# Second attention of a two-layer transformer kernel: softmax row sums taken beside the exponentials, 16 reciprocals a row, and two steps of VectorE's order moved

## The chip, the cores and the metric

One Trainium2 chip, one of its cores. The metric is the device time of one execution in microseconds (us); smaller is better. The kernel before was timed three times: 2356.11 us in the median, 2355.34 the lowest and 2362.7 the highest.

## The reference

Two layers work on 2048 tokens of 512 channels, each layer an attention and a feed-forward, each with a layer norm modulated by a conditioning vector. The first feed-forward is a mixture of 64 experts, 8 of them per token. The change is in the attention of the second layer:

```python
# q: 16 heads of 32; k, v: 4 heads of 32, each shared by 4 query heads; q and k get a rotary embedding
for qs in range(0, S, WINDOW):            # WINDOW = 128 queries
    # keys: 16 meta tokens, and the window of 128 positions up to the query
    scores = einsum('bhqd,bhkd->bhqk', q_c, k_c) * scale
    scores = where(allowed, scores, -inf)
    attn = softmax(scores, axis=-1)
    chunks.append(einsum('bhqk,bhkd->bhqd', attn, v_c))
...
return y @ Wo + bo
```

The softmax is computed as exp(s - max) and divided by its sum over the keys. All is float32.

## The kernel before, in words

The kernel is one program of several stages; the second attention is a block of its own between two barriers. It works on 16 tiles ("rows") of 128 tokens. Each engine has a hand-written program with one function `turn` that `schedule(turn)` (L1369) calls 22 times, once per m from -4 to 17. In turn m seven different rows are in work at once: `g=m+4` gathers the expert outputs from memory, `y=m+3` adds them to the residual `x_res` and takes the statistics of the layer norm, `p=m+2` is normalised and projected, `f=m+1` has its queries and keys transposed, `s=m` gets scores, masks, minima and exponentials, `a=m-1` has its probabilities transposed and multiplied with the values, `w=m-2` is normalised by the row sums, projected by Wo and added to the residual. A row index outside 0 to 15 is None and its part is left out. There is no planner: within a turn each engine runs its list in the order written, and semaphores tie the engines together.

VectorE (L1714), per turn: `xhat` (L1720, needs GpSimd's 1/sqrt of the variance, L1457); the normalisation of row w (L1725 a RECIPROCAL of the 128x512 sums from PSUM, L1727 the product with the output, which gives `o_out`); quarter 0 of the minima of row s (`maxima(s,0)`, four L1690 and one L1694, which writes the differences for the meta keys); the keys' copy (L1737); three experts added (L1701); the query bias (L1746, waits for the projection, gives `q_rows`); quarter 1; two experts; the bias of keys and values (L1756, L1758); quarter 2; three experts; the residual sum of row w (L1767, `x_out`); quarter 3; the statistics of row y (L1703: L1708, L1710, L1712, each behind a small memset, L1656).

GpSimd (L1454), per turn: L1457; the modulation of h (L1417 and L1461, gives `h_done`); L1465 (`x_res` plus bias); gathers of three experts of row g (each L1445, an indirect DMA that GpSimd issues, behind one small L1422); the rotary embedding of the queries (L1417, L1437; waits for `q_rows`); two gathers; the rotary embedding of the keys; three gathers. Before each group of gathers it waits for `y_sum`, that is until VectorE has added the same experts of the row before (L1442), because they are read from the same buffer.

TensorE (L1559), per turn: scores of quarter 0 (L1546); the transposes of h (L1569, wait for `h_done`) and of the queries (L1576); the transposes of the probabilities of quarter 0 of row a (L1556, wait for `o_out`, since they use the banks that held the output and the sums); the query projection (L1590, its end starts L1746); scores 1, transposes 1, key and value projection (L1599), scores 2, transposes 2, the Wo projection (L1610), transposes 3, scores 3, the transposes of the meta probabilities (L1622), the transposes of the keys (L1630, wait for `x_out`), and last the two products of row a: values times probabilities into bank `b_o`, ones times probabilities (the row sums, spread over 32 partitions per head) into bank `b_sum`. Each product is 8 matmuls of 512 columns (L1639) and 16 of 128 columns (L1643); the second set has the same shapes and another left operand.

ScalarE (L1501) copies PSUM to SBUF (hT L1506, qT L1511, the transposed probabilities L1499, the meta ones L1518, kT L1528) and takes the exponentials, 16 per row of 256 columns (L1492), after each quarter of the minima, and one for the meta keys (L1534). SyncE loads the tables of the rotary embedding (L1409) two rows ahead.

Of the kernel before, what the change touches and what calls it, by code (L numbers as in the profile page):

```python
# [5 lines left out]
ALU = mybir.AluOpType  # L6
# [103 lines left out]
def adaln_two_layers(nc, a, out):  # L110
    ctx = ExitStack()
    with ctx:
# [1207 lines left out]
        with ExitStack() as ph, nc.Block() as block:  # L1320
# [17 lines left out]
            meta_sum = cv(HP, 2, HD)  # L1338
            ones_f = cv(HD)
# [6 lines left out]
            nmx = cv(2, NHEAD)  # L1346
            spare = cv(2)
            free = mod[:, 0].rearrange("p j c -> p (j c)")
            oT, osum = free[:, 0:C].rearrange("p (r n) -> p r n", r=HP), free[:, C:2 * C]
# [8 lines left out]
                     "exp_done", "meta_exp", "pT_mm", "pT_out", "pM_mm", "pM_out", "o_mm", "o_out", "wo_mm", "x_pre", "x_out",  # L1358
# [3 lines left out]
             exp_done, meta_exp, pT_mm, pT_out, pM_mm, pM_out, o_mm, o_out, wo_mm, x_pre, x_out,  # L1362
# [3 lines left out]
            ba, bb, b_o, b_sum = psum[6], psum[7], psum[4], psum[5]  # L1366
# [48 lines left out]
            def _(pool):  # L1415
# [34 lines left out]
                st.did(nc.gpsimd.memset(ones_f, 1.0))  # L1450
# [33 lines left out]
            def _(act):  # L1484
                copy = nc.scalar.copy

                def exps(t, c):
                    for r in range(HP):
                        n = HP * c + r
                        act.wait_ge(mx_done, NHEAD * t + n + 1)  # L1490
                        some = slot(t, c)[:, r, META:KEYS1]
                        nc.scalar.activation(some, some, ACT.Exp, bias=nmx[:, t % 2, n:n + 1], scale=-1.0).then_inc(exp_done, 1)  # L1492
# [8 lines left out]
                def turn(g, y, p, f, s, a, w):  # L1501
                    if p is not None:
# [35 lines left out]
            def _(pe):  # L1538
# [20 lines left out]
                def turn(g, y, p, f, s, a, w):  # L1559
                    if s is not None:  # L1560
                        scores(s, 0)
                    if p is not None:
# [3 lines left out]
                        if a:  # L1566
                            pe.wait_ge(pM_out, a)
# [10 lines left out]
                    if f == 0:  # L1578
                        pe.wait_ge(spread_done, 1)
                        pe.wait_ge(kv_rows, 1)  # L1580
                        nc.tensor.matmul(b_sum[:, 0:NKV1 * HD], spread, v[0:META, 0].rearrange("p h d -> p (h d)"), start=True, stop=True).then_inc(meta_mm, 1)
# [34 lines left out]
                    if a is not None:  # L1616
                        pe.wait_ge(meta_exp, a + 1)
                        pe.wait_ge(kv_rows, p + 1 if p is not None else NT)
                        if a:
                            pe.wait_ge(pM_out, a)  # L1620
                        for n in range(2):
                            mm = nc.tensor.transpose(bb[:, n * P:(n + 1) * P], prob_meta[:, a % 2, HM * n:HM * n + HM].rearrange("p h k -> p (h k)"), ident[:])  # L1622
                        mm.then_inc(pM_mm, 1)
# [8 lines left out]
                    if a is not None:  # L1632
                        pe.wait_ge(pT_out, copies_before(a + 1, 0))
                        pe.wait_ge(pM_out, a + 1)
                        for bank, local, meta in ((b_o, lambda k, c: v[:, keys_of(a, k) % VRING, c], lambda r, c: v_meta[:, c // 2, r, c % 2]),
                                                  (b_sum, lambda k, c: ones_f, lambda r, c: meta_sum[:, r, c % 2])):
                            for k in chunks(a):
                                for c in range(NKV1):
                                    nc.tensor.matmul(bank[HD * c:HD * c + HD], local(k, c), probT[:, k, c].rearrange("p r n -> p (r n)"),  # L1639
                                                     start=(k == 0), stop=False)  # L1640
                            for r in range(HP):
                                for c in range(NKV1):
                                    mm = nc.tensor.matmul(bank[HD * c:HD * c + HD, r * P:(r + 1) * P], meta(r, c), metaT[:, c // 2],  # L1643
                                                          start=False, stop=(r == HP - 1))
                                    if r == HP - 1:
# [539 lines left out]
```

## Time and profile before

| | us |
|---|---|
| median of 3 runs (lowest, highest) | 2356.11 (2355.34, 2362.7) |
| the profiled execution, its own time | 2370.22 |
| its span in the profile | 2366.9 |
| second attention, from its first xhat to its last residual sum | 1241 to 1775 |
| TensorE busy over the span | 2059.5 (87%) |
| VectorE, GpSimd, ScalarE busy over the span | 1122.9, 726.6, 708.0 |
| mean granted TensorE clock, share of 2.4 GHz | 0.935 |

The table is read from the page of the profile (its first part has the busy times) and from the timelines of the block. A busy share averages over stages with different limits, so this case is read row by row inside the one stage: which wait ends last in a row, and what the engine that ended it had been doing. "Idle before <- X" in a line names the instruction whose end released the wait. A wait marked "issue" ended with nothing that the profile can name; where a semaphore had several sources it can still be one of them, and the ends of the other engines' instructions show which. Granted clock 1.00 is 2.4 GHz, 0.50 is 1.2 GHz.

### The profile page before, as it was taken

The page shows a single profiled execution, that of the slowest core. Times are in us where ns is not written, and L with a number is a line of the kernel's source. Part 1 is how long each engine was busy: PE and PEld are TensorE (multiplying, and loading weights), DVE is VectorE, ACT ScalarE, POOL GpSimd, SP SyncE. Part 2 cuts the span into 40 slices and gives each one's busy share as a digit, 9 for nine tenths or more (in the row PEclk, how much of TensorE's full clock was granted, in tenths as well). Part 3 has the DMA queues.
Part 4 walks back from the last instruction along what each step waited for, and adds up shares of the span by engine and source line. Part 5 has one row for each costly group of instructions (what it writes and reads, how often), then busy time and mean ns, then how long its engine had stood idle before and what let it go on. Part 6 is the DMA issues. An engine that isn't in the chain of part 4 may idle for free. (4 is left out here: it accounts for less than half of the span.)

```text
span 2366.9 us, 39347 instructions
## 1 busy us (share of the span) xinstructions
PE 2059.5 (87%) x11764; PEld 1340.5 (57%) x11766; DVE 1122.9 (47%) x2920; ACT 708.0 (30%) x1455; POOL 726.6 (31%) x1164
## 2 busy tenths in 40 slices
PE   4799877999999999999933788888875999999998
PEld 2677544555555555555511445545543878878787
DVE  2466666555553222222225677777534444443432
ACT  0233235222222222222200444444522332232221
POOL 0243302223333333233337666666302101101000
PEclk7799889999999999999966799999987999999999
DMA  7565632566555566656552222222002112121210
GB/s 249 178 212 202 218 115 81 190 197 196 181 192 189 181 220 201 212 183 220 166 164 74 74 74 74 79 73 71 1 1 72 63 62 72 63 80 62 80 63 27
DMA packets 122555, 302.36 MB, mean 128 GB/s; under 512 B 24912, under 2 KB 28624, under 8 KB 122320
## 3 DMA queue, kind: packets, MB, share of 16 engines
q1 hardware_dynamic: 73424, 179.04, 22.4%
q0 software_dynamic: 23040, 75.52, 11.4%
q10 hardware_dynamic: 25984, 46.38, 5.3%
q8 instruction: 67, 1.10, 0.2%
q14 instruction: 40, 0.33, 0.0%
HBM read 216.47 MB, written 83.36 MB: 127 GB/s over the span
## 5 line engine op out<-in xcount | busy, mean ns | idle before, releaser
L1166 PE MATMUL bank<-arena 128*128 x1272 | 445.6, 494 | 9.9 <-issue 8.8
L1166 PEld LDWEIGHTS bank<-arena 128*128 128x128 f32 x1272 | 229.6, 190 | 147.6 <-issue 16.9
L1183 PE MATMUL bank<-arena 96*128 x632 | 297.5, 593 | 0.2 <-issue 0.2
L1287 DVE TENSOR_TENSOR arena<-bank,mod 128x512 f32<-128x512 f32 x158 | 109.2, 691 | 215.4 <-PE bank L1183 176.7
L1881 PE MATMUL bank<-x_hi,w_hi 128*128 128x512 f32 x512 | 200.9, 392 | 6.0 <-DVE x_lo L2014 6.0
L1881 PE MATMUL bank<-x_hi,w_lo 128*128 128x512 f32 x512 | 199.4, 389 | 0.0
L1881 PE MATMUL bank<-x_lo,w_hi 128*128 128x512 f32 x512 | 199.2, 389 | 0.0
L1282 DVE TENSOR_TENSOR arena<-arena,bank 128x192 f32<-128x192 f32 x159 | 56.3, 354 | 300.9 <-ACT arena L1204 300.4
L1199 ACT COPY arena<-bank 96x256 f32<-96x256 f32 x158 | 58.1, 368 | 424.0 <-issue 221.9
L1145 POOL DMA_INDIRECT arena<-h_moe,arena x160 | 158.2, 989 | 75.3 <-issue 74.0
L1144 POOL TENSOR_TENSOR arena<-neg_half 128x1 f32<-128x1 f32 x160 | 31.4, 196 | 462.8 <-PE bank L1175 462.6
L2094 DVE SCALAR_TENSOR_TENSOR ffn_arena<-bank,ffn_arena,mod 128x512 f32<-128x512 f32 x64 | 48.0, 751 | 221.3 <-PE bank L1881 174.3
L1183 PEld LDWEIGHTS bank<-arena 96*128 96x128 f32 x632 | 107.3, 190 | 76.4 <-issue 76.4
L1445 POOL DMA_INDIRECT route_hot<-y_moe,pos_u x128 | 125.5, 981 | 32.1 <-issue 27.9
L1701 DVE SCALAR_TENSOR_TENSOR x_res<-route_hot,route_w,x_res 128x512 f32<-128x512 f32 x128 | 115.4, 902 | 25.5 <-DMA route_hot<-y_moe,pos_u 17.7
L1862 POOL TENSOR_TENSOR ffn_arena<-ffn_arena,neg_half 128x1 f32<-128x1 f32 x16 | 8.8, 548 | 386.3 <-DVE ffn_arena L2028 386.3
L1492 ACT ACTIVATE arena<-arena 128x256 f32<-128x256 f32 x256 | 109.2, 502 | 18.7 <-DVE arena L1690 18.6
L1175 PEld LDWEIGHTS bank<-ident,arena 128*128 128x128 f32 x640 | 80.2, 141 | 58.9 <-issue 28.7
L1881 PEld LDWEIGHTS bank<-x_hi,w_hi 128*128 128x128 f32 x512 | 96.1, 188 | 29.0 <-issue 4.8
L1556 PE MATMUL bank<-ident,arena 128*128 128x128 f32 x496 | 78.4, 309 | 34.3 <-issue 31.9
L1881 PEld LDWEIGHTS bank<-x_hi,w_lo 128*128 128x128 f32 x512 | 96.1, 188 | 20.2
L1881 PEld LDWEIGHTS bank<-x_lo,w_hi 128*128 128x128 f32 x512 | 96.2, 188 | 19.4
(318 smaller groups left out, 3679.4 us busy)
## 6 DMA issues: line engine op xcount, KB each, us to landing
arena<-in_moe_up SPq DMA_DIRECT2D x64, 768.0 KB, 7.9
y_moe<-arena ACTq DMA_DIRECT2D x158, 256.0 KB, 2.9
y_moe<-mod SPq DMA_DIRECT2D x32, 1024.0 KB
ffn_arena<-in_ffn_up SPq DMA_DIRECT2D x64, 512.0 KB, 3.3
arena<-in_moe_down SPq DMA_DIRECT2D x64, 384.0 KB, 9.9
arena<-in_L_wmod SPq DMA_DIRECT2D x12, 1024.0 KB, 6.5
x_res<-in_L_attn_x SPq DMA_DIRECT2D x1, 4096.0 KB
h_moe<-arena SPq DMA_DIRECT2D x16, 256.0 KB, 7.3
```

The costliest lines, as they stand in the source:

```text
L1145: nc.gpsimd.indirect_dma_start(out=xg[:, b], out_offset=None, in_=h_moe, in_offset=bass.IndirectOffsetOnAxis(ap=st_tok[:, b], axis=0)).the ...
L1166: mm = nc.tensor.matmul(psum[2 + b][:, 0:2 * FI], xgT[:, b, k], up_ring[:, bass.ds((e % RING) * UPW + k * 2 * FI, 2 * FI)], start=(k == 0) ...
L1175: mm = nc.tensor.transpose(psum[b][:, k * P:(k + 1) * P], xg[:, b, k * P:(k + 1) * P], ident[:])
L1183: mm = nc.tensor.matmul(psum[6 + b][:], hiddenT[:, b, n], down_ring[:, bass.ds((e % RING) * DOWNW + n * C, C)], start=(n == 0), stop=(n == 1))
L1199: nc.scalar.copy(hiddenT[:, b], psum[4 + b][0:FH, 0:2 * P].rearrange("p (n q) -> p n q", n=2)).then_inc(hT_out, 1)
L1282: nc.vector.tensor_tensor(hidden[:, b], gate_act[:, b], psum[2 + b][:, FI:2 * FI], ALU.mult).then_inc(hidden_done, 1)
L1287: nc.vector.tensor_tensor(y[:, b], psum[6 + b][:], mod[:, 0, 5], ALU.mult).then_inc(y_out, 1)
L1445: nc.gpsimd.indirect_dma_start(out=yg[:, j], out_offset=None, in_=y_moe, in_offset=bass.IndirectOffsetOnAxis(ap=pos_u[:, t, j:j + 1], axis ...
L1492: nc.scalar.activation(some, some, ACT.Exp, bias=nmx[:, t % 2, n:n + 1], scale=-1.0).then_inc(exp_done, 1)
L1556: mm = nc.tensor.transpose(psum[4 + k][:, r * P:(r + 1) * P], slot(t, c)[:, r, at:at + P], ident[:])
L1701: nc.vector.scalar_tensor_tensor(x_res[:, t], yg[:, j], route_w[:, t, j:j + 1], x_res[:, t], ALU.mult, ALU.add).then_inc(y_sum, 1)
L1881: mm = nc.tensor.matmul(bank, x, y, start=(n == 0), stop=(n == len(passes) - 1))
```

## The change

Six edits, all in the block of the second attention:

1. TensorE no longer computes the row sums: the second product (8 L1639 and 16 L1643 a row) is gone, with the tiles `ones_f` and `meta_sum`.
2. ScalarE's exponentials give their sum along the keys through `accum_out` into `esum`, 16 a row.
3. VectorE has a new step `sums(a)` between the query bias and quarter 1: a reduce of the meta probabilities (128x256 to 128x16), an add of 128x16 and a reciprocal of 128x16, which gives `r_done`. Row w loses its 128x512 reciprocal.
4. The 16 reciprocals a token are turned by one more TensorE transpose (into the bank of the meta transposes), copied by ScalarE (`rT`), spread by four TensorE matmuls with a selection matrix `sel` (16 partitions, 128 columns each) into bank `b_r` ahead of the product with the values, and copied by ScalarE into `rb` at the start of the next turn. L1727 then multiplies the output with `rb`.
5. VectorE's residual sum of row w (L1767) stands before the last three experts and no longer behind them.
6. The statistics of row y stand before quarter 3 of the minima and no longer behind it.

Cut to its core:

```diff
@@ ScalarE
                 def exps(t, c):
+                    if t >= 2 and c == 0:
+                        act.wait_ge(r_done, t - 1)
...
-                        nc.scalar.activation(some, some, ACT.Exp, bias=nmx[:, t % 2, n:n + 1], scale=-1.0).then_inc(exp_done, 1)
+                        nc.scalar.activation(some, some, ACT.Exp, bias=nmx[:, t % 2, n:n + 1], scale=-1.0,
+                                             accum_out=esum[:, t % 2, n:n + 1]).then_inc(exp_done, 1)
...
                 def turn(g, y, p, f, s, a, w):
+                    if w is not None:
+                        act.wait_ge(o_mm, 2 * NKV1 * w + HP)
+                        if w:
+                            act.wait_ge(o_out, w)
+                        copy(rb, b_r[:]).then_inc(rb_out, 1)
...
                                 act.wait_ge(pM_mm, a + 1)
+                                copy(rT, bb[0:NHEAD, 2 * P:3 * P]).then_inc(pM_out, 1)
@@ TensorE
+                        pe.wait_ge(r_done, a + 1)
+                        nc.tensor.transpose(bb[0:NHEAD, 2 * P:3 * P], rinv, ident[:]).then_inc(pM_mm, 1)
...
-                        for bank, local, meta in ((b_o, lambda k, c: v[:, keys_of(a, k) % VRING, c], lambda r, c: v_meta[:, c // 2, r, c % 2]),
-                                                  (b_sum, lambda k, c: ones_f, lambda r, c: meta_sum[:, r, c % 2])):
+                        for r in range(HP):
+                            nc.tensor.matmul(b_r[:, r * P:(r + 1) * P], sel[:, r], rT, start=True, stop=True).then_inc(o_mm, 1)
...
@@ VectorE
+                def sums(t):
+                    dve.wait_ge(meta_exp, t + 1)
+                    dve.wait_ge(exp_done, NHEAD * t + NHEAD)
+                    if t:
+                        dve.wait_ge(pM_mm, t)
+                    st.did(nc.vector.tensor_reduce(msum, prob_meta[:, t % 2], AX.X, ALU.add))
+                    st.settle()
+                    st.did(nc.vector.tensor_tensor(msum, msum, esum[:, t % 2], ALU.add))
+                    st.settle()
+                    nc.vector.reciprocal(rinv, msum).then_inc(r_done, 1)
...
-                        st.did(nc.vector.reciprocal(osum, b_sum[:]))
-                        st.settle()
-                        nc.vector.tensor_tensor(oT.rearrange("p r n -> p (r n)"), b_o[:], osum, ALU.mult).then_inc(o_out, 1)
+                        dve.wait_ge(rb_out, w + 1)
+                        nc.vector.tensor_tensor(oT.rearrange("p r n -> p (r n)"), b_o[:], rb, ALU.mult).then_inc(o_out, 1)
...
+                    if a is not None:
+                        sums(a)
                     if s is not None:
                         maxima(s, 1)
...
                     if s is not None:
                         maxima(s, 2)
-                    if y is not None:
-                        for j in range(5, TOPK):
-                            add_expert(y, j)
                     if w is not None:
                         dve.wait_ge(wo_mm, w + 1)
                         dve.wait_ge(x_pre, w + 1)
                         nc.vector.tensor_tensor(x_res[:, w], ba[:], x_res[:, w], ALU.add).then_inc(x_out, 1)
+                    if y is not None:
+                        for j in range(5, TOPK):
+                            add_expert(y, j)
+                    if y is not None:
+                        statistics(y)
                     if s is not None:
                         maxima(s, 3)
-                    if y is not None:
-                        statistics(y)
```

Once per execution, `sel` is filled by a VectorE copy of 512 columns, and the copy of as many columns that filled `meta_sum` is gone.

## Rows read from the trace of the kernel before

**Rows 1.** Windows, one for each row between two L1746; engine busy (instructions), clock, DMA share, GB/s.

```profile
1361.94:1391.56 29.62, 24.85 (x202) 14.29 (x203) 22.34 (x58) 13.15 (x29) 19.41 (x24) 0.94 0.27 74
...
1624.79:1653.26 28.47, 25.02 (x202) 14.83 (x203) 21.91 (x58) 13.21 (x29) 19.49 (x23) 0.94 0.28 77
```

**Rows 2.** VectorE timeline, one row: start, us, instruction, [idle before <- what released it].

```profile
1506.22 0.69 DVE L1746 TENSOR_TENSOR arena<-bank,arena 128x512 f32<-128x512 f32 x1 [1.23 <-PE bank L1590]
...
1508.55 2.17 DVE L1694 TENSOR_TENSOR mod<-arena 128x64 f32<-128x64 f32 x1
...
1517.92 0.68 DVE L1767 TENSOR_TENSOR x_res<-bank,x_res 128x512 f32<-128x512 f32 x1
...
1526.53 3.36 DVE L1725 RECIPROCAL mod<-bank 128x512 f32<-128x512 f32 x1 [2.72 <-PE bank L1643]
```

**Rows 3.** TensorE timeline of the same row.

```profile
1518.75 0.63 PE L1630 MATMUL bank<-ident,arena 128*128 128x128 f32 x4 [2.10 <-DVE x_res L1767]
...
1530.71 1.94 PE L1556 MATMUL bank<-ident,arena 128*128 128x128 f32 x8 [2.64 <-issue]
```

**Rows 4.** GpSimd timeline of the same row.

```profile
1518.80 0.19 POOL L1422 TENSOR_TENSOR arena<-neg_half 128x1 f32<-128x1 f32 x1
...
1525.25 1.27 POOL L1461 TENSOR_TENSOR down_scale<-down_scale,mod 128x512 f32<-128x512 f32 x1
```

**Rows 5.** Timeline, VectorE, GpSimd and TensorE, an early row without residual sum.

```profile
1328.13 1.12 PE L1569 MATMUL bank<-ident,down_scale 128*128 128x128 f32 x4 [5.67 <-POOL down_scale L1461]
...
1335.05 0.69 DVE L1746 TENSOR_TENSOR arena<-bank,arena 128x512 f32<-128x512 f32 x1 [4.18 <-PE bank L1590]
...
1344.83 0.43 DVE L1690 CUSTOM_DVE_ANT_0 arena<-bank,mask 128x272 f32<-128x272 f32 x1
...
1345.30 0.46 POOL L1437 TENSOR_TENSOR arena<-arena,mod 128x128 f32<-128x128 f32 x1
...
1353.46 1.11 PE L1569 MATMUL bank<-ident,down_scale 128*128 128x128 f32 x4 [1.57 <-POOL down_scale L1461]
```

**Rows 6.** Timeline, the next row: VectorE's L1694 beside GpSimd's pair of L1417.

```profile
1363.77 1.65 POOL L1417 TENSOR_TENSOR mod<-arena 128x256 f32<-128x256 f32 x2
...
1364.26 1.25 DVE L1694 TENSOR_TENSOR mod<-arena 128x64 f32<-128x64 f32 x1
```

**Rows 7.** Timeline, late rows, without gathers: TensorE, VectorE, GpSimd.

```profile
1668.90 1.27 POOL L1461 TENSOR_TENSOR down_scale<-down_scale,mod 128x512 f32<-128x512 f32 x1
...
1673.94 1.94 PE L1556 MATMUL bank<-ident,arena 128*128 128x128 f32 x8 [2.62 <-issue]
...
1690.87 1.92 PE L1639 MATMUL bank<-arena 128*32 128x512 f32 x16
...
1695.17 1.08 PE L1643 MATMUL bank<-arena 128*32 128x128 f32 x32
...
1696.37 3.36 DVE L1725 RECIPROCAL mod<-bank 128x512 f32<-128x512 f32 x1 [4.51 <-PE bank L1643]
...
1764.89 3.36 DVE L1725 RECIPROCAL mod<-bank 128x512 f32<-128x512 f32 x1 [6.75 <-PE bank L1643]
```

**Rows 8.** Groups of instructions that come nearest to the added ones.

```profile
L1233 DVE TENSOR_REDUCE arena<-arena 128x4 f32<-128x256 f32 x16 | 6.7, 421 | 0.5
...
L700 DVE RECIPROCAL arena<-bank 128x8 f32<-128x8 f32 x32 | 4.4, 179 | 2.1 <-PE bank L595 2.1
...
L691 DVE TENSOR_TENSOR route_w<-arena 128x16 f32<-128x16 f32 x8 | 1.3, 167 | 0.0
...
L1492 ACT ACTIVATE arena<-arena 128x256 f32<-128x256 f32 x256 | 109.2, 502 | 18.7 <-DVE arena L1690 18.6
...
L1518 ACT COPY arena<-bank 128x256 f32<-128x256 f32 x16 | 6.0, 373 | 5.5 <-PE bank L1622 5.0 <-issue 0.4
```

**Rows 9.** Timeline, TensorE: matmuls from 16 partitions, and of 256 columns.

```profile
1275.83 0.79 PE L1581 MATMUL bank<-arena 16*128 16x128 f32 x2
...
1507.72 1.89 PE L1599 MATMUL bank<-arena,mod 128*128 128x256 f32 x8
```

More of the change, by code:

```diff
@@ L1345, in adaln_two_layers @@
             st1, r1 = cv(8), cv(2)
-            nmx = cv(2, NHEAD)
+            nmx, esum = cv(2, NHEAD), cv(2, NHEAD)
+            msum, rinv = cv(NHEAD), cv(NHEAD)
+            rT, sel = cv(P)[0:NHEAD], cv(HP, P)[0:NHEAD]
             spare = cv(2)
             free = mod[:, 0].rearrange("p j c -> p (j c)")
-            oT, osum = free[:, 0:C].rearrange("p (r n) -> p r n", r=HP), free[:, C:2 * C]
+            oT = free[:, 0:C].rearrange("p (r n) -> p r n", r=HP)
+            rb = free[:, C:2 * C]
             hT = free[:, 2 * C:3 * C].rearrange("p (k n) -> p k n", k=KC)
@@ L1580, in turn @@
                         pe.wait_ge(kv_rows, 1)
-                        nc.tensor.matmul(b_sum[:, 0:NKV1 * HD], spread, v[0:META, 0].rearrange("p h d -> p (h d)"), start=True, stop=True).then_inc(meta_mm, 1)
+                        nc.tensor.matmul(b_r[:, 0:NKV1 * HD], spread, v[0:META, 0].rearrange("p h d -> p (h d)"), start=True, stop=True).then_inc(meta_mm, 1)
                     if a is not None:
@@ L1633, in turn @@
                         pe.wait_ge(pT_out, copies_before(a + 1, 0))
-                        pe.wait_ge(pM_out, a + 1)
-                        for bank, local, meta in ((b_o, lambda k, c: v[:, keys_of(a, k) % VRING, c], lambda r, c: v_meta[:, c // 2, r, c % 2]),
-                                                  (b_sum, lambda k, c: ones_f, lambda r, c: meta_sum[:, r, c % 2])):
[L1637 to L1645, printed above, removed]
-                                        mm.then_inc(o_mm, 1)
+                        pe.wait_ge(pM_out, 2 * a + 2)
+                        for r in range(HP):
+                            nc.tensor.matmul(b_r[:, r * P:(r + 1) * P], sel[:, r], rT, start=True, stop=True).then_inc(o_mm, 1)
+                        for k in chunks(a):
+                            for c in range(NKV1):
+                                nc.tensor.matmul(b_o[HD * c:HD * c + HD], v[:, keys_of(a, k) % VRING, c], probT[:, k, c].rearrange("p r n -> p (r n)"),
+                                                 start=(k == 0), stop=False)
+                        for r in range(HP):
+                            for c in range(NKV1):
+                                mm = nc.tensor.matmul(b_o[HD * c:HD * c + HD, r * P:(r + 1) * P], v_meta[:, c // 2, r, c % 2], metaT[:, c // 2],
+                                                      start=False, stop=(r == HP - 1))
+                                if r == HP - 1:
+                                    mm.then_inc(o_mm, 1)
                 schedule(turn)
@@ L1661, in weights_ready @@
                     st.did(nc.vector.tensor_tensor(bo, bo, mod[:, 1, 2], ALU.mult))
+                    st.did(nc.vector.tensor_copy(sel.rearrange("n r (c d) -> n r c d", c=NKV1),
+                                                 ident[0:NHEAD, 0:NHEAD].rearrange("n (c r) -> n r c", r=HP).unsqueeze(3).to_broadcast([NHEAD, HP, NKV1, HD])))
                     nc.vector.tensor_copy(spread.rearrange("p (h k) -> p h k", h=HM),
@@ L1670, in meta_values @@
                     head = meta_head.rearrange("p (c r) -> p r c", c=2).unsqueeze(3).to_broadcast([P, HP, 2, HD])
-                    st.did(nc.vector.tensor_copy(meta_sum[:], head))
                     dve.wait_ge(meta_mm, 1)
                     for n in range(2):
-                        rows = b_sum[:, n * 2 * HD:(n + 1) * 2 * HD].rearrange("p (c d) -> p c d", c=2)
+                        rows = b_r[:, n * 2 * HD:(n + 1) * 2 * HD].rearrange("p (c d) -> p c d", c=2)
                         st.did(nc.vector.tensor_tensor(v_meta[:, n], rows.unsqueeze(1).to_broadcast([P, HP, 2, HD]), head, ALU.mult))
```

16 lines of the change are left out of this document (6 added, 10 removed).

## The prediction, made before the result was known

> **What bounds the kernel now.** I first cut the block into rows of work, from one start of the query bias L1746 to the next, and asked for busy times [rows 1]. The 10 rows from 1361.94 to 1653.26 take 291.3 us, 29.13 each. No engine is busy all the time: TensorE some 25 us, VectorE 22, GpSimd 19, ScalarE 13. So a row is bound by a chain that hops between engines, and a removed instruction is worth what it had on that chain. The clock column is 0.94 to 1.00.
>
> The timelines of one row show the chain [rows 2 to 4]. VectorE reaches L1767 at 1517.92, behind three experts; TensorE had waited 2.10 us for it before the keys' transposes at 1518.75; both products follow; at 1526.53 VectorE starts the 3.36 us reciprocal, after 2.72 us of waiting for the products. TensorE's next transposes start at 1530.71 after 2.64 us of idle that the view calls "issue"; the end of L1727 (right behind the reciprocal, 0.7 us) is what they waited for. Then come the query projection and the next L1746. Beside it runs a second chain: GpSimd issues three gathers from 1518.80 and finishes the modulated h at 1525.25 + 1.27 = 1526.52 [rows 4]. That is just when the products end. That is the point of this case: who comes second decides what the removal is worth.
>
> The early rows, before any output exists, show the second chain alone [rows 5]. From h at 1328.13 TensorE needs 6.92 us to the query bias at 1335.05; VectorE has added its last expert at 1344.83; GpSimd ends the keys' rotation at 1345.76, gathers, and h of the next row is there at 1353.46. That is 25.3 us with no reciprocal in it, with half the transposes of a full row.
>
> After 1653 there are no gathers, and the rows are bound by TensorE and the reciprocal [rows 7].
>
> **Part by part.** All sums are against the profiled execution, 2370.22 us (span 2366.9). It is 14.1 above the median of 2356.11; I take the differences over unchanged.
>
> Removed: the reciprocal, 3.36 plus some 0.04 of settling, 3.4 a row on VectorE. The second product: both take 1695.17 + 1.08 - 1690.87 = 5.4 us undisturbed [rows 7], half of it, 2.6 to 2.7, goes; in rows with gathers the same stretch lasts from 1519.3 to 1526.5, 7.2 [rows 2, 3], so up to 1 us more may go there.
>
> Added on TensorE: one transpose and four matmuls from 16 partitions. L1581 is that kind: 2 instructions of 128 columns in 0.79 at the 1.2 GHz level [rows 9]. L1599, at 2.4 GHz, has 8 of 256 columns in 1.89, so 8 of 128 take 0.9. Bounds 0.9 and 1.6; I take 0.9, as the stretch runs mostly at 2.4 GHz. The products become 0.9 + 2.6 = 3.5 instead of 5.4.
>
> Added on ScalarE: a copy of 128 columns ahead of the meta one. L1518, twice as wide, takes 0.37 [rows 8], so 0.25; it lies on the path to the products, which hence gain 1.9 - 0.3 = 1.6, I take 1.5. A copy of 512 columns at the turn's start, 0.6, is hidden in the 28 us row with 13 busy. The sums of the 16 exponentials: the trace has no activation with an accumulator. VectorE's own read of one costs 0.08; the exponential takes 0.50. Bounds 0 and 0.4 each; I take 0.15, 2.4 us a row, nearest VectorE's read. That is hidden with gathers; in the late rows it makes the exponentials catch up with the transposes' copies, some 0.6 in two rows.
>
> Added on VectorE: sums(a), 0.42 + 0.17 + 0.18 [rows 8] and settling, 0.9. It has a second price. It starts right after L1746, when GpSimd begins its pair of L1417, and its add reads two SBUF operands like L1694. L1694, alone some 0.2 as L691, took 1.25 there and ended with the pair at 1365.5 [rows 6], 2.17 in another row [rows 2]. So I let the add wait until the pair ends: 1.8 for sums(a), bounds 0.9 and 2.8. The Trainium skill, in SBUF (State Buffer), section "Who interferes with whom", says that a VectorE instruction with two SBUF inputs blocks on a GpSimd one that reads SBUF, that the holder keeps the port for one whole instruction, and that a reduce never contends. The trace agrees on who contends, but L1694 was held over two instructions, not one; by the rule sums(a) would cost 1.1 and the total would be some 7 us lower. The measurement decides.
>
> Moved: L1767 before the last three experts. It would be ready earlier by three experts, but TensorE's other work (scores 3, meta transposes) ends 2.10 before it gets L1767's result [rows 3], so 2.1 at most is gained on that chain. And the last three experts, with them GpSimd's last three gathers, come later by L1767's 0.7. The statistics before quarter 3 gain nothing with gathers, as L1457 stands behind the gathers in GpSimd's queue. Behind sums(a) in VectorE's queue stand quarter 1, 5 experts and L1767, so the gathers are late by 1.8 more. SyncE's queue isn't touched; the sel copy replaces the meta_sum copy, 0.
>
> **The sum, rows with gathers.** First chain: L1746 to the end of the products was 1526.5 - 1506.2 = 20.3; now 20.3 - 2.0 - 1.5 = 16.8, then L1727 0.7, transposes 1.9 and projection 3.8, twice L1599 [rows 3, 9]: 23.2. Second chain: from L1746 to the last expert 9.78 [rows 5], plus 0.7 and 1.8, is 12.3; GpSimd's gathers up to h 1526.52 - 1518.80 = 7.7; a hop 0.1; from h to L1746 6.92 with four transposes, 0.9 more with eight, 7.9 (1361.94 - 1353.46 = 8.5 is the bound above, 6.9 the one below). Total 28.0. It is now the longer one by almost 5 us: 29.13 - 28.0 = 1.1 a row, 11 over ten rows. The row at 1335 has sums(a) without the rest: its last expert at 11.6 against GpSimd's 10.7, a loss of 0.9.
>
> **The sum, late rows.** The first (L1746 at 1653.26) still waits for h, at 1670.17 before; the transposes started at 1673.94 and now can some 0.8 behind h, after L1569 and L1576: 3.0. Then four products, 1.5 each, 6.0, and four reciprocals (1696.37 to 1764.89), 3.4 each, 13.6; ScalarE takes back 1.2. With TensorE's shorter idles some transposes stay at 2.4 GHz; L1556 took 1.94 there after 2.62 of idle, half of that at 2.4 GHz: I take 1.5 over the late rows, bounds 0 and 4. Together 3.0 + 6.0 + 13.6 - 1.2 + 1.5 = 23.
>
> **Total** 11 - 0.9 + 23 = 33: 2337 in the profiled execution, 2356.1 - 33 = **2323** in the median. Later stages lie behind a barrier and shift whole.
>
> **Rivals.**
> (a) GpSimd's queue, not the sum's add, is the limit: the add slips between GpSimd's instructions and experts overlap the rotation. The row is then the early one plus four transposes, 25.3 + 0.9 = 26.2, 2.9 saved, 29 in ten rows and the 0.9 not lost: 52 with the late rows, 2304. For: the early rows ran like this. Against: 9.8 + 0.7 + 0.9 already exceeds GpSimd's 10.7.
> (b) The accumulator costs 0.4 each: 4 us a row more; the late rows become bound by ScalarE, which takes back 5 more: 2328. Against: VectorE's 0.08.
> (c) TensorE waits longer for h, about 4 us a row instead of 1.8 to 2.6, and runs the whole stretch from h to L1746 at 1.2 GHz: L1569 1.1, L1576 1.1, L1556 1.9 and the projection twice 3.8, 11.7 less overlaps, 11 instead of 7.9. Row 31.1, a loss of 2.0, 20 in ten rows, against the late 23 less 0.9: 2354, no change. Against: in the early row, after 5.67 of idle, projection and all came in 6.92 [rows 5].
> (d) **Slower:** VectorE and GpSimd hold each other up all along the longer queue before the gathers: sums(a) 2.8 instead of 1.8, two L1694 at 2.2 instead of some 0.2 to 0.4, 3.8, together 4.8: the last expert 17.1 after L1746 instead of 12.3; then 17.1 + 7.8 + 8.5 = 33.4, 4.3 lost a row, 43 + 0.9 - 23 = +21: 2377. It decides from a last expert 15.7 us after L1746 on (a loss of 2.9 a row, 7 in all). For: 2.17 for L1694 happened [rows 2]. Against: with it, L1746 to L1767 was 11.7.
> Should the change's sums not replace the second product, nothing of the time would move except through the order; the diff leaves no room for that.
>
> **The numbers.** Forecast 0.55, (a) 0.18, (b) 0.10, (c) 0.10, (d) 0.07. Changes within 0.3%, 7 us, are about what a measurement of this kernel can't tell from none. (a), (b) and the forecast are faster: 0.83; (c) same 0.10; (d) slower 0.07. The forecast's own bounds: gather rows 27.0 to 29.1 (21 to 0 saved), late 20 to 25, so 2311 to 2337. To hold 8 in 10 the range reaches to (a) and over (b), and part of the way to (c): 2302 to 2344.
>
> **What would show it.** Rows with gathers of 28.0 between L1746s, TensorE idle 3 to 5 us before L1569 with GpSimd's L1461 as releaser, GpSimd's last L1422 waiting for VectorE's L1701; L1725 gone; products of 3.5; late rows near 18.5 instead of (1764.89 - 1696.37)/3 = 22.8. GpSimd's L1422 without that wait and rows of 26 say (a); ScalarE's accumulator reads name (b). The forecast is wrong if rows with gathers stay over 29, or if TensorE's wait before L1556 still ends with L1727.

## The result, and the profile after

| | before | after |
|---|---|---|
| median (lowest, highest), 4 runs each | 2357.02 (2355.34, 2362.7) | 2319.49 (2316.85, 2322.45) |
| the profiled execution, its own time | 2370.22 | 2322.45 |
| its span | 2366.9 | 2320.6 |
| second attention, first xhat to end of the last residual sum | 533.9 | 489.7 |
| ten rows between query biases, with gathers | 29.13 each | 27.53 each |
| from the last of these biases to the end | 121.9 | 95.8 |

Ratio 0.9837, 95% interval 0.9815 to 0.9859: 37.5 us faster, where 33 was predicted. A second measurement of the unchanged source later gave 0.9793 (0.9778 to 0.9809), 49.9 us; there the kernel before had a median of 2366.78. The two intervals do not meet. Within the profiled executions the block lost 44.2 us, and the rest of the span 2.1.

The busy times on the page:

```profile
PE 2024.3 (87%) x11149; PEld 1332.4 (57%) x11150; DVE 1095.3 (47%) x2952; ACT 742.9 (32%) x1743; POOL 725.6 (31%) x1163
```

TensorE gave up 35 us, VectorE 28, and ScalarE took on 35. None of the three is the 44 of the block, so the rows have to be read. The last of the ten windows from one query bias to the next, columns as in [rows 1]:

```profile
1606.85:1634.59 27.74, 22.69 (x163) 14.12 (x163) 21.70 (x59) 15.57 (x47) 17.12 (x20) 0.94 0.25 72
```

Again no engine is busy throughout. The clock column is 0.88 or 0.94 in the ten windows, where before it was 0.89 in one, 0.94 in seven and 1.00 in two. VectorE's timeline of one row, which answers to [rows 2]:

```profile
1497.94 0.69 DVE L1767 TENSOR_TENSOR arena<-bank,arena 128x512 f32<-128x512 f32 x1 [4.13 <-PE bank L1599]
1498.55 0.41 DVE L1713 TENSOR_REDUCE arena<-mod 128x16 f32<-128x256 f32 x1
1498.99 0.67 DVE L1715 TENSOR_TENSOR arena<-arena 128x16 f32<-128x16 f32 x1
1499.70 0.25 DVE L1717 RECIPROCAL arena<-arena 128x16 f32<-128x16 f32 x1
...
1507.25 2.58 DVE L1723 SCALAR_TENSOR_TENSOR x_res<-route_hot,route_w,x_res 128x512 f32<-128x512 f32 x3
...
1514.83 0.69 DVE L1748 TENSOR_TENSOR mod<-bank,mod 128x512 f32<-128x512 f32 x1
```

L1767 is the query bias (1746 before), L1748 the product with the reciprocals, with nothing in front of it any more, L1723 an expert. Three things show: the bias waited 4.13 us for TensorE; the sums L1713 to L1717 take 1.3 us in all; L1748 waits for nobody (it follows the xhat step, ahead of which VectorE had idled 1.64 us for GpSimd). Now GpSimd and TensorE of the same row:

```profile
1498.78 1.67 POOL L1418 TENSOR_TENSOR mod<-arena 128x256 f32<-128x256 f32 x2 [1.00 <-issue]
...
1509.91 0.19 POOL L1423 TENSOR_TENSOR arena<-neg_half 128x1 f32<-128x1 f32 x1 [0.63 <-DVE x_res L1723]
...
1516.34 1.26 POOL L1461 TENSOR_TENSOR down_scale<-down_scale,mod 128x512 f32<-128x512 f32 x1
```

```profile
1489.99 1.11 PE L1578 MATMUL bank<-ident,down_scale 128*128 128x128 f32 x4 [3.70 <-POOL down_scale L1461]
1490.89 1.06 PE L1585 MATMUL bank<-ident,arena 128*128 128x128 f32 x4
1491.75 1.91 PE L1565 MATMUL bank<-ident,arena 128*128 128x128 f32 x8
1493.45 4.45 PE L1599 MATMUL bank<-arena,mod 128*128 128x512 f32 x8
...
1509.33 1.12 PE L1646 MATMUL bank<-arena 16*128 16x128 f32 x8 [0.26 <-ACT arena L1527]
1510.38 1.92 PE L1649 MATMUL bank<-arena 128*32 128x512 f32 x16
1512.12 1.06 PE L1653 MATMUL bank<-arena 128*32 128x128 f32 x32
1513.11 0.74 PE L1555 MATMUL bank<-arena 32*128 32x272 f32 x8
1517.65 0.66 PE L1578 MATMUL bank<-ident,down_scale 128*128 128x128 f32 x4 [3.80 <-POOL down_scale L1461]
...
1519.83 4.91 PE L1599 MATMUL bank<-arena,mod 128*128 128x512 f32 x8
```

This is the chain that was forecast: last expert ends 11.9 after the bias, GpSimd's last group of gathers waits for it, h is ready at 1516.34 + 1.26 = 1517.60, 19.66 after the bias, and TensorE had been idle for 3.80. The spread and the products take 1513.1 - 1509.3 = 3.8 where both products took 7.2 [rows 2, 3]. After an idle of 3.70 the transposes run as at 1.2 GHz: 1.11 and 1.91, where [rows 3] have 1.94 at that level; the projection takes 4.45, the first part of it slow. After the next idle, of 3.80, the transposes of h still take 0.66, and it is the projection that is slow, 4.91. The ten rows have both kinds: from h (the end of L1461) to the bias it takes some 8.0 or 7.2, and 8.4 in the first of them. Further down, a stretch without such an idle will have 0.66, 1.04 and 3.60 for the same three.

Late rows, VectorE, which answer to [rows 7]:

```profile
1673.25 0.69 DVE L1748 TENSOR_TENSOR mod<-bank,mod 128x512 f32<-128x512 f32 x1 [3.25 <-PE bank L1653]
...
1690.26 0.69 DVE L1748 TENSOR_TENSOR mod<-bank,mod 128x512 f32<-128x512 f32 x1 [3.26 <-PE bank L1653]
```

The steady late rows last 17.01, 16.87 and 18.07, 17.3 in the mean, against 22.8 before and 18.5 predicted. (In the change's second profiled execution the third of them took 15.21.)

### The profile page after: what moved, and what is told of

It is laid out like the page before. It is cut to its first block and busy times, and to the rows that moved or that the text cites. A ratio compares the mean times of both kernels' runs of the same rounds, so it can differ in the third digit from the quotient of the medians.

```text
span 2320.6 us, 38481 instructions
## 1 busy us (share of the span) xinstructions
PE 2024.3 (87%) x11149; PEld 1332.4 (57%) x11150; DVE 1095.3 (47%) x2952; ACT 742.9 (32%) x1743; POOL 725.6 (31%) x1163
## 5 line engine op out<-in xcount | busy, mean ns | idle before, releaser
L1494 ACT ACTIVATE arena<-arena 128x256 f32<-128x256 f32 x256 | 127.0, 500 | 44.9 <-DVE arena L1701 44.6
L1723 DVE SCALAR_TENSOR_TENSOR x_res<-route_hot,route_w,x_res 128x512 f32<-128x512 f32 x128 | 112.8, 881 | 26.6 <-DMA route_hot<-y_moe,pos_u 18.0
L1578 PE MATMUL bank<-ident,down_scale 128*128 128x128 f32 x64 | 14.6, 369 | 124.0 <-POOL down_scale L1461 124.0
## 6 DMA issues: line engine op xcount, KB each, us to landing
x_res<-in_L_attn_x SPq DMA_DIRECT2D x1, 4096.0 KB, 18.5
```

Of the source, the lines that this page charges most:

```text
L1723: nc.vector.scalar_tensor_tensor(x_res[:, t], yg[:, j], route_w[:, t, j:j + 1], x_res[:, t], ALU.mult, ALU.add).then_inc(y_sum, 1)
```

## The experiments

They ran in three groups, each on a chip of its own, and each with the kernel before beside it (2366.33, 2366.78 and 2367.4 in the median). So ratios are compared, not microseconds; the first four experiments are one group, the last three another. "Rows" is the mean of the ten rows with gathers, "block" the second attention.

| | ratio (95%) | rows | block |
|---|---|---|---|
| order alone | 0.9956 (0.9942, 0.9970) | 27.98 | 520.7 |
| old order | 0.9748 (0.9731, 0.9764) | 26.28 | 477.3 |
| sums early | 0.9762 (0.9745, 0.9778) | 26.85 | 482.4 |
| product twice | 0.9807 (0.9790, 0.9824) | 26.35 | 484.9 |
| the change, again | 0.9793 (0.9778, 0.9809) | 27.26 | 487.1 |
| filler | 0.9747 (0.9731, 0.9762) | 26.08 | 473.4 |
| sums and experts first | 0.9727 (0.9703, 0.9752) | 25.71 | 470.8 |
| the same with one filler | 0.9732 (0.9714, 0.9750) | 26.32 | 471.3 |
| no accumulator | 0.9805 (0.9786, 0.9824) | 27.31 | 484.9 |
| filler, copy late | 0.9736 (0.9719, 0.9754) | 26.19 | 471.9 |
| filler, copy late, sums early | 0.9734 (0.9715, 0.9754) | 26.11 | 472.6 |

Two theories stood against each other at first: that a row ends with the last expert, GpSimd's gathers and h, whatever TensorE does; and rival (c) in a wider form, that TensorE's idle before h sets a good part of the time behind h, through the clock.

**Order alone.** In the kernel before, the residual sum goes ahead of the last three experts, and the statistics ahead of quarter 3 (edits 5 and 6 of the diff, nothing else).

> The kernel before with the two moves in VectorE's order alone (residual sum before the last three experts, statistics before quarter 3); reciprocal and second product stay. My theory: in the kernel before the chain that ends a row with gathers is residual sum, products, reciprocal, and GpSimd's chain ends just with it. The move gives the first up to 2.1 us and makes the second 0.7 later, so rows with gathers fall from 29.1 to 28.5 (28.0 to 29.0), the late rows keep 22.8 but for one that wins up to 1: ratio to before 0.997 (0.993 to 1.000). Rival, the order is what brought the gain of the change: rows with gathers at 27.5, ratio 0.992 or less.

Rows of 27.98, at the lower end of what was expected, and 13 us less in the block (534 to 521). So the order alone is worth 13 us of the block as long as the reciprocal is there. It can't be added to the rest, as the next run shows.

**Old order.** The whole change, but the residual sum and the statistics where they were.

```diff
-                    # residual sum(w); experts 5 to 7; statistics(y); maxima(s, 3)
+                    # experts 5 to 7; residual sum(w); maxima(s, 3); statistics(y)
```

> The changed kernel with VectorE's old order (last three experts, residual sum, quarter 3, statistics). My theory: rows with gathers are now bound by the last expert, the three gathers behind it and h. The last experts come 0.7 earlier, TensorE's products come up to 2 us later but have 3.7 us of idle behind them. So rows with gathers take 27.0 instead of 27.5 (26.7 to 27.5), the one late row that waits for the statistics loses 1 to 2: same as the changed kernel or faster by up to 4 us, ratio to before 0.983 (0.980 to 0.985). Rival, the move matters: rows with gathers back over 28.5, ratio 0.988 or more.

The expectation missed: rows of 26.28, not 26.7 to 27.5. It is faster than the complete change, by more than was thought, with intervals that don't meet (0.9748 here, 0.9793 for the change in the next group, on another chip). TensorE in one of its rows:

```profile
1450.88 0.63 PE L1640 MATMUL bank<-ident,arena 128*128 128x128 f32 x4 [2.45 <-DVE x_res L1790]
...
1452.55 3.53 PE L1649 MATMUL bank<-arena 128*32 128x512 f32 x16
...
1458.69 0.66 PE L1578 MATMUL bank<-ident,down_scale 128*128 128x128 f32 x4 [1.07 <-POOL down_scale L1461]
...
1460.49 3.60 PE L1599 MATMUL bank<-arena,mod 128*128 128x512 f32 x8
```

The idle of 2.45 us now lies before the products, which run slowly (3.53 instead of 1.92), but they are not on the longer chain. The work behind h, which is, runs at 2.4 GHz: from h to the bias 5.50, against 7.2 to 8.4 in the change. In this row h came 20.8 after the bias, later than the change's 19.66, and it still was shorter. Over the ten rows the granted clock is 0.89, not higher than the change's 0.91: the slow stretch is still there, but lies where it costs nothing. So the order's move, which helps with the reciprocal, costs time without it. The two moves were not run apart. In the row shown the statistics end at 1453.45, before GpSimd comes to use them at 1454.77, so they release nothing there, and the difference lies with the residual sum.

**Sums early.** `sums(a)` ahead of the query bias, while VectorE waits for it anyway.

```diff
+                    if a is not None:
+                        sums(a)
                     if p is not None:
                         dve.wait_ge(q_mm, p + 1)
```

> The changed kernel with sums(a) ahead of the query bias, where VectorE waits 3.3 to 4.5 us for TensorE. My theory: sums(a) is 1.3 us of the chain that bounds rows with gathers, and GpSimd's queue is only 1.3 us away (it waits 0.63 twice for VectorE); rows with gathers fall from 27.5 to 26.4 (26.1 to 26.8), late rows win 0 to 1 each: 11 to 14 us below the changed kernel, ratio to before 0.978 (0.976 to 0.980). Rival, the rows are bound by GpSimd's own queue or TensorE's clock: no difference, 27.5, ratio 0.984.

1.3 us left the queue before the gathers, but the last expert moved from 11.9 to 11.63 only, because VectorE now came to the residual sum before its projection was there:

```profile
1500.24 0.69 DVE L1787 TENSOR_TENSOR x_res<-bank,x_res 128x512 f32<-128x512 f32 x1 [1.40 <-PE bank L1619]
```

The moved residual sum is thus a bound of its own. Rows were 26.85, just above the expected 26.4 (26.1 to 26.8). Of the 0.41 us a row that this is under the second execution of the change (27.26, below), 0.11 is h being earlier in the mean (0.3 in most rows, but 1.2 later in one), and 0.30 is a shorter time behind h: two rows have 5.50 there.

**Product twice.** TensorE does the product with the values twice, into the same bank. The first theory gives 3 us more work no price with gathers.

```diff
+                        for again in range(2):
                         # the 8 L1649 and 16 L1653; o_mm in the second pass only
```

> The changed kernel with the product of the values done twice into the same bank, so the second product's time is back on TensorE with nothing else changed. My theory: in rows with gathers TensorE idles 3.7 us behind the products, so up to 3.6 more cost nothing on the second chain; rows stay at 27.5 (27.3 to 28.3); in four late rows 2.6 each come back, 10.4 us. Ratio to before 0.988 (0.987 to 0.992). Rival, the products are still on the chain in rows with gathers: rows of 30, 25 us more on top, ratio 0.999.

```profile
1508.59 3.05 PE L1650 MATMUL bank<-arena 128*32 128x512 f32 x15
...
1514.26 0.66 PE L1578 MATMUL bank<-ident,down_scale 128*128 128x128 f32 x4 [0.64 <-POOL down_scale L1461]
1514.75 0.60 PE L1585 MATMUL bank<-ident,arena 128*128 128x128 f32 x4
1515.19 1.04 PE L1565 MATMUL bank<-ident,arena 128*128 128x128 f32 x8
1516.06 3.60 PE L1599 MATMUL bank<-arena,mod 128*128 128x512 f32 x8
```

More work made these rows shorter: 26.35, not 27.5 or more. The idle shrinks from 3.8 to between 0.5 and 1.0, the granted clock over the ten rows is 1.00 instead of 0.91, and from h to the bias it takes 5.49, against 7.6 in the mean of the change, although h comes only at 20.7 to 21.2. In the late rows, where TensorE is the bound, the same work costs what it takes: 19.60 and 19.47 instead of 17.01 and 16.87. This run decides between the two theories: idle, and the clock after it, is worth about 2 us of each of these rows behind h. One us of that is lost again ahead of h; the filler run shows to what. In the total nothing is left of it: against the change's second execution the ten rows have 9.0 us less and the late part 9.3 more, and the ratio is 0.9807 beside the change's 0.9793.

**The change again**, beside the next three.

> The changed kernel once more, on the same chip as the three beside it. Rows with gathers 27.5 between two query biases, ratio to before 0.982 (0.980 to 0.985) by every theory.

Rows of 27.26, and a ratio of 0.9793, just under the range. TensorE's idle before h was 2.4 here, with 7.18 or 7.98 behind h by turns. The last expert was again at 11.9 and h at 19.7.

**Filler.** Three matmuls of 512 columns into a free bank, just before TensorE waits for h, behind the scores of quarter 0 and once ScalarE has copied the keys out of that bank. They compute nothing that is used.

```diff
+                    if a and p is not None and p < NT - 1:
+                        pe.wait_ge(k_in, f)
+                        for again in range(3):
+                            nc.tensor.matmul(ba[:], wo[:, 0, 0:P], wo[:, 1], start=True, stop=True)
                     if p is not None:
                         pe.wait_ge(h_done, p + 1)
```

> The changed kernel with three matmuls of 512 columns into the free bank ba while TensorE waits for h, in the rows with gathers (2.6 us of 3.8 idle). Their result is overwritten. My theory after the product done twice: h is ready 19.7 after the query bias as before, and TensorE, at 2.4 GHz, then needs 5.5 instead of 7.2 to 8.1 for the transposes and the query projection: rows of 25.2 (25.1 to 25.6), 22 us less than the changed kernel in ten rows, ratio to before 0.973 (0.971 to 0.976). Rival: it was not the clock that made rows with the product done twice shorter, but where TensorE's work falls against the others; then the rows stay at 27.5, ratio 0.982.

The window over the block, of the change (first) and of this kernel:

```profile
1240.00:1731.00 491.00, 376.80 (x2522) 230.39 (x2522) 330.44 (x937) 244.69 (x750) 299.81 (x347) 0.87 0.22 64
```

```profile
1242.00:1717.00 475.00, 392.31 (x2588) 230.62 (x2588) 330.62 (x937) 240.51 (x750) 306.14 (x347) 0.92 0.24 66
```

TensorE was busy for 15.5 us more, and the block was 16 shorter: the mean clock went from 0.87 to 0.92, and over the ten rows from 0.91 to 1.00. (Against the change's second execution, on the same chip, also at 0.87 and 0.91, it is 8.0 us more and 13.7 shorter.) From h to the bias it is 5.50 in every row with gathers, as expected. But rows are 26.08, not 25.2, since h is ready only 20.58 after the bias; the ratio, 0.9747, fell in its range. GpSimd and VectorE:

```profile
1507.78 0.59 POOL L1457 TENSOR_TENSOR arena<-arena,neg_half 128x1 f32<-128x1 f32 x1
...
1515.61 0.19 POOL L1423 TENSOR_TENSOR arena<-neg_half 128x1 f32<-128x1 f32 x1 [2.73 <-DVE x_res L1727]
```

```profile
1511.03 0.70 DVE L1709 TENSOR_TENSOR mod<-arena 128x64 f32<-128x64 f32 x1
1511.65 1.51 DVE L1762 COPY arena<-arena 128x512 f32<-128x512 f32 x1
1513.08 2.45 DVE L1727 SCALAR_TENSOR_TENSOR x_res<-route_hot,route_w,x_res 128x512 f32<-128x512 f32 x3
```

A third loop has become the bound: GpSimd's first gathers of a row wait for VectorE's third expert, and behind them GpSimd's queue runs without a gap (bar its own issue) to the next L1457 at 1533.86, 18.2 us later and 26.08 after the one shown; that starts the next xhat. Neither the bias nor TensorE is in it here. The same queue without a gap stands in the product twice: 18.3 us from the first gathers to L1457, after a wait of 3.07 for the third expert, which is why h came late there. L1762, a copy that takes 0.42 undisturbed, took 1.51. What stood beside it is not the modulation of h, as a later expectation says, which ended at 1511.64, but the GpSimd instruction behind it (L1465, `x_res` plus bias, 1511.60 to 1512.87).

**Sums and experts first**, without and with one filler matmul. Sums early, and the last three experts ahead of the residual sum, which the runs above had shown as a bound.

> The changed kernel with sums(a) ahead of the query bias and the last three experts before the residual sum. In the run with sums(a) early VectorE waited 1.4 for the Wo projection ahead of the residual sum, so the experts behind it gained nothing. Theory: with the experts first they end 10.3 to 11.1 after the query bias, GpSimd's queue (10.7) becomes the limit, h is there at 18.4 to 19.0; then 5.5 at 2.4 GHz or 7.2 at the lower level: rows of 24.2 (23.9 to 25.6). Ratio to before 0.970 (0.966 to 0.976). Rival, the order of residual sum and experts does not matter once the sums are early: 26.8 as in the run with sums early, ratio 0.976.

> The kernel beside it (sums early, experts first) with one matmul of 512 columns while TensorE waits for h. [...] Ratio to before 0.968 (0.965 to 0.972).

Without filler, two rows of 23.9 and 24.0 came out as expected (h at 18.4, then 5.50), but others took up to 27.8; the mean of 25.71 is above the expected range. Two kinds of rows, TensorE before h:

```profile
1535.94 0.80 PE L1578 MATMUL bank<-ident,down_scale 128*128 128x128 f32 x4 [3.31 <-POOL down_scale L1461]
...
1561.51 0.66 PE L1578 MATMUL bank<-ident,down_scale 128*128 128x128 f32 x4 [2.07 <-POOL down_scale L1461]
```

After 3.31 of idle the bias came 7.17 behind h, after 2.07 it came 5.50 behind (but 6.94 in another row with 2.06); h itself came between 18.4 and 20.7 after the bias. With the one filler matmul the idle is gone in most rows, the rows take 25.4 to 27.2, and the ratio of 0.9732 is the same within the intervals, outside the expected 0.965 to 0.972. In six of the ten rows TensorE came to h 1.4 to 1.5 us after it was ready, with 1.1 of the filler ahead of it: a filler that ends after h is ready is itself in the way.

**Filler, copy late**, without and with sums early. The keys' copy goes behind the first three experts, to shorten the third loop.

```diff
+                        for j in range(0, 3):
+                            add_expert(y, j)
                     # the copy of the keys (L1758), then no experts 0 to 2
```

> The changed kernel with the three matmuls in TensorE's wait for h, and with the keys' copy (L1758, 1.51 us when it meets GpSimd's modulation of h, 0.42 otherwise) behind the first three experts and not ahead of them. With the filler alone rows took 26.08, not 25.2: theory, a third loop bounds them, GpSimd's queue without a gap from the first gathers to 1/sqrt (18.2), xhat (0.6), and VectorE's 7.1 from xhat to the third expert, 26.0 together; L1758 is 1.5 of it. So rows fall to 25.2 (24.7 to 25.5), where the second chain takes over (19.7 + 5.5): ratio to before 0.970 (0.968 to 0.973). Rival: GpSimd is delayed by sharing the memory port with VectorE, the copy only moves to where it meets the gathers, and rows stay at 26.0.

> The same with sums(a) ahead of the query bias. Second chain 19.4 + 5.5 = 24.9, third loop 24.5, VectorE no longer idle ahead of the query bias. Rows of 24.9 (24.5 to 25.3), ratio to before 0.969 (0.966 to 0.972); against the run beside it 0 to 5 us less. If VectorE itself becomes the limit, its sums push the query bias and rows are 25.5 or more.

```profile
1502.64 4.54 PE L1574 MATMUL bank<-arena 128*128 128x512 f32 x6
...
1503.79 1.26 POOL L1461 TENSOR_TENSOR down_scale<-down_scale,mod 128x512 f32<-128x512 f32 x1
```

```profile
1505.06 3.47 DVE L1727 SCALAR_TENSOR_TENSOR x_res<-route_hot,route_w,x_res 128x512 f32<-128x512 f32 x3
1508.45 0.42 DVE L1765 COPY arena<-arena 128x512 f32<-128x512 f32 x1
```

Both missed: 26.19 and 26.11 instead of 25.2 and 24.9. The copy is back to 0.42, but the three experts that took its place, beside L1465 behind GpSimd's h, need 3.47 instead of 2.45 (the first 1.76, the other two 0.75 each), so most of the wait only changed its owner. And in every third row or so the fillers ran slowly, 4.54 instead of 2.84, and ended 2 us behind h: those rows took 27.3 to 27.6, the others 25.1 to 26.1. The rival's number, 26.0, is near, but the copy did not move to a place where it is held.

**No accumulator.** `accum_out` is left out of the exponentials; the row sums are then read from a tile that nothing fills.

> The changed kernel without accum_out in the 16 exponentials of a row: the sums are read from a tile that nothing fills. An exponential of the changed kernel starts 0.49 after the one before, of the kernel before 0.40, so each accumulator costs ScalarE 0.09, 1.4 a row. In rows with gathers that is hidden: 27.3 as with it. In the late rows of 17.0, 12 exponentials stand between the first and last transposes of a row: 0.3 to 1.1 a row shorter in two of them, 1 to 3 us in all. Ratio to before within 0.002 of the changed kernel's 0.979. Rival: the accumulators bound the rows with gathers through the last copies ahead of the products; then 0.5 to 1.4 a row less there.

ScalarE of the change, and of this kernel:

```profile
1500.30 0.51 ACT L1494 ACTIVATE arena<-arena 128x256 f32<-128x256 f32 x1
1500.72 0.19 ACT L1494 ACTIVATION_READ_ACCUMULATOR arena<-arena 128x1 f32 x1
1500.81 0.49 ACT L1494 ACTIVATE arena<-arena 128x256 f32<-128x256 f32 x1
```

```profile
1499.84 1.71 ACT L1494 ACTIVATE arena<-arena 128x256 f32<-128x256 f32 x4
```

The read of 0.19 overlaps; from one start to the next it is 0.49 with it, and without it four take 1.71, about 0.40 each. So 0.09 an exponential, 1.4 us a row, and it is hidden: rows 27.31, late rows 17.01 and 16.67 against 17.01 and 16.87, ratio 0.9805 against 0.9793.

**The kernel before again**, one execution, to see how far one profile can be trusted.

> The kernel before once more, for a second profile. From the first xhat of the block to its last residual sum 534 us in the first profile; the ten rows with gathers 29.1 each. I expect both within 2 us and 0.2 a row if one profile of it is enough to compare with.

2367.62 us, block 534.3 against 533.9, rows 29.04 against 29.13, as expected.

No run takes out the reciprocal and leaves the second product, so their shares in the rows with gathers are told apart by the traces alone.

## Why the prediction was right, by its steps

**The total.** 33 predicted, 37.5 measured in the medians. By the profiled executions, against which the sum was made, it is 44 in the block: 16.0 in ten rows (predicted 11), 1.9 in the row at 1334 (predicted a loss of 0.9), 26.1 in the late part (predicted 23). All three were short, in one direction, and the medians hid part of that: the profiled execution of before was 13.2 above its median, that of after 3.0. So it is partly luck that the medians came within 5 us. Why the kernel before ran some 10 us shorter in its first, unprofiled executions than in all later ones, no trace shows; that stays open (they may have been on another chip than the profile). By the later ratio of 0.9793 the forecast would have been 16 us too high, but inside the range.

**The second chain** was right in each of its stations: last expert 11.9 (12.3), GpSimd's last gathers waiting for it, h at 19.66 (12.3 + 7.7 = 20.0, the difference being the expert's), the releaser GpSimd's L1461, idle 3.7 to 5.0 (3 to 5), from h to the bias 7.2 to 8.4, 7.6 in the mean (7.9). The row came to 27.53 where 28.0 stood in the sum. VectorE's 3.36 us reciprocal is gone and no wait took its place before the product. The prediction's reading of the clock column as 0.94 to 1.00 was wrong for the very row of [rows 2 to 4], which has 0.89; no term of the sum hung on it.

**sums(a)** was sized 1.8 and took 1.3. Its add took 0.67 (0.18 in the product twice, where GpSimd was issuing gathers beside it) and ended with the first instruction of GpSimd's pair, not with the pair, as I had taken from L1694 in [rows 6]. The rule of the Trainium skill, SBUF (State Buffer), section "Who interferes with whom", that the holder keeps the port for one whole instruction, was nearer here: 1.1 by it. That the reduce is not held, which it also says, the trace shows too (0.41, as in [rows 8]). But in the same row L1705 (L1694 before) took 0.69 instead of 0.23 beside h, and the keys' copy 1.51 instead of 0.42 right behind it, so the holds are real, and rival (d) had them right in kind and wrong in size: a last expert at 11.9 against its 17.1.

**The row at 1334.** The loss by sums(a) is there: h is done 19.46 after the bias, where it was 18.36. But from the first transpose of h to the bias it is 5.44, where it was 8.48. Two lines of before, then two of after:

```profile
1355.49 1.94 PE L1556 MATMUL bank<-ident,arena 128*128 128x128 f32 x8
1357.22 4.68 PE L1590 MATMUL bank<-arena,mod 128*128 128x512 f32 x8
```

```profile
1354.75 1.04 PE L1565 MATMUL bank<-ident,arena 128*128 128x128 f32 x8
1355.62 3.60 PE L1599 MATMUL bank<-arena,mod 128*128 128x512 f32 x8
```

The reciprocal stood close to this chain: L1727 behind it ended at 1355.39, just ahead of the first of these lines. But TensorE started that line 0.06 us behind its work before it, so next to nothing was waited for. The 3 us are that the same matmuls ran slowly before (1.94 and 4.68) and did not after, although the idle ahead of h was alike, 1.57 and 1.68; the change's own slow rows take 8.0 in this stretch without any reciprocal. The failed step is "sums(a) without the rest": the stretch behind h was taken as unchanged. In the second profile of the kernel before the reciprocal held the same transposes by 0.9, and the stretch was 8.21. What sets the level in this row stays open.

**Late rows.** 17.3 instead of 18.5: three times 1.2 covers the 3 us. ScalarE took nothing back (0.09 an exponential, not 0.15, and hidden), which is some 0.6 in two rows; most of the rest stands in TensorE's speed, most of all in the last such row (the first three groups of transposes 1.07, 1.64 and 1.94 instead of three times 1.94). From VectorE's first instruction behind the last product to the block's end it was 5.2 instead of 10.2: 3.4 of it the reciprocal, 1.66 the Wo projection, which now has 0.89 of idle ahead of it and not 4.26:

```profile
1769.03 5.36 PE L1610 MATMUL bank<-arena,mod 128*128 128x512 f32 x8 [4.26 <-DVE mod L1727]
```

```profile
1725.94 3.70 PE L1619 MATMUL bank<-arena,mod 128*128 128x512 f32 x8 [0.89 <-DVE mod L1748]
```

(Before, and after.) The spread cost 1.1 (0.9 taken), and with the 0.26 wait for ScalarE's copy the products stand at 3.8 (3.5 taken).

**Rivals.** (b) fell with 0.09. (a), GpSimd's queue as the limit, fell in this kernel (GpSimd does wait 0.63), and came true once the fillers had removed the rest: rows of 26.08, near the 26.2 it gave, but that the number fits is chance, since it came by a loop over the third expert that I had not drawn. (c), the clock, was a real mechanism that I priced as a rival and partly had in the sum: its idle of about 4 us came, and it costs the change 1.7 to 2.9 us a row (7.2 to 8.4 against 5.50), but the stretch did not run at the lower level from end to end, so it was not the rival's 11. What I missed altogether is that the moved residual sum is what places TensorE's idle ahead of h.

**Best version.** Sums and experts first, with or without a filler, and the filler with the late copy: 0.9727 to 0.9736. The filler alone has 0.9747 and the old order 0.9748, and the intervals of all of these overlap, so none is shown to be the best. All beat both kernels; the simplest is the old order.

## What to carry to other kernels

When an instruction leaves the longer of two chains, the price is the distance to the second one, and that second chain can be read in the trace of before, station by station, in a stretch where the first is not yet active. Two edits that are each good beside the old bound need not be good together: after the first, ask again where the idle of the next engine falls. On TensorE, an idle ahead of critical work cost more than itself here, so put waits ahead of work that has slack, and take the row that the change is in, not its neighbour.

## What was not expected of the hardware

- Added work on TensorE made rows shorter: 3 us of second product, rows 27.3 to 26.4. The stretch from h to the bias takes 7.2 to 8.4 after 3.7 to 5.0 of idle and 5.5 after 0.5 to 1.0. The slow part falls on its start (the 4 transposes of h take 1.11 instead of 0.66) or only on the projection behind it (4.91 instead of 3.60, after transposes of 0.66). After an idle of 2.4 it was 7.2 to 8.0 in the change's second execution and 5.50 in two rows of the early sums, so the length of the idle alone does not settle it.
- A copy of 128x512 from SBUF to SBUF on VectorE took 1.51 instead of 0.42 beside a GpSimd add of 128x512, and of three fused multiply-adds the first took 1.76 instead of 0.75 beside the same.
- A ScalarE activation that also gives its sum cost 0.09 us more than without (128x256), though its read shows as 0.19.
